# Reordering VectorE's part of a delta-rule step, and moving a gate from GpSimd to VectorE, in a one-core attention and experts kernel

## The reference

```python
def step(S, inp):                       # S: [b, h, 16, 16], 8 x 16 = 128 of them
    qt, kt, vt, at, gkt = inp
    S = S * jnp.exp(gkt)[..., None]
    sab = jnp.einsum('bhk,bhkv->bhv', at, S)
    S = S + kt[..., None] * (sab[..., None, :] + vt[..., None, :])
    ot = jnp.einsum('bhk,bhkv->bhv', qt, S)
    return (S, ot)
...
_, o = jax.lax.scan(step, S0, seq)      # 512 steps, one after the other
...
o = o * jax.nn.sigmoid(x @ Wog1 @ Wog2) # the gate of the outputs
...                                     # layer norm of o, @ Wo
out = out + cw[:, e:e + 1] * y          # eight experts, top 2 of each token
...
g = _silu(_L0_ffn_ref(xn, ...))
x = x + s * g
```

## Time and profile before

| | |
|---|---|
| runs | 1128.91, 1129.39, 1130.73 us; median 1129.39 us |
| profiled execution | 1127.93 us, of which the span of its instructions 1126.2 us |
| VectorE busy | 1067.1 us, 95% of the span |
| GpSimd busy | 924.9 us, 82% |
| TensorE busy | 898.2 us, 80% |
| ScalarE busy | 462.3 us, 41% |
| chain that ended last | VectorE 67%, issue 14%, GpSimd 9% |

### The profile page before, as it was taken

The page is one execution under the profiler, slowest core; times in us unless marked ns, Lnnn a source line. Parts: engine busy times, 40 slices in busy tenths (PEclk is TensorE's granted clock), DMA queues, the critical chain, the costliest instruction groups (busy, mean ns, idle before and its releaser), DMA issues.

```text
span 1126.2 us, 17298 instructions
## 1 busy us (share of the span) xinstructions
PE 898.2 (80%) x3893; PEld 703.1 (62%) x3893; DVE 1067.1 (95%) x3292; ACT 462.3 (41%) x1182; POOL 924.9 (82%) x921
## 2 busy tenths in 40 slices
PE   5899979312539999999989999999999962687761
PEld 3444434112528888888878888888888852566641
DVE  3899999999999999999999999999999999999994
ACT  5878858400003333333333333333333310788761
POOL 3887757447766899999989999999999998999993
PEclk9989979655769999999999999999999985888985
DMA  5656566666235767766767776666666615556322
GB/s 160 199 178 226 177 204 199 227 189 199 90 113 151 214 210 219 212 195 203 216 177 219 215 219 210 203 200 213 212 206 204 199 42 150 161 158 196 102 69 65
DMA packets 238292, 202.76 MB, mean 180 GB/s; under 512 B 140528, under 2 KB 216272, under 8 KB 238224
## 3 DMA queue, kind: packets, MB, share of 16 engines
q1 hardware_dynamic: 161184, 82.93, 27.4%
q10 hardware_dynamic: 70224, 100.49, 26.9%
q0 software_dynamic: 6816, 18.69, 4.7%
HBM read 139.54 MB, written 62.54 MB: 179 GB/s over the span
## 4 chain that ended last, share of the span: by engine, by line
DVE 67%; issue 14%; POOL 9%; SPq 4%; DMA 3%; PE 2%; ACT 1%; DVEq 0%; POOLq 0%; ACTq 0%
DVE obh L1324 9%; DVE psB L1382 7%; DVE state L1398 6%; DVE ubuf L1387 5%; DVE outer L1395 5%; DVE psB L1385 5%; DVE psB L1393 5%; POOL prod_a L370 3%; DVE ubuf L1340 3%; POOL prod_q L387 3%; DVE prod_a L1333 3%; DVE prod_q L1388 2%; DVE psB L1390 2%; SPq L395 2%; DMA rec_d<-work 2%
## 5 line engine op out<-in xcount | busy, mean ns | idle before, releaser
L370 POOL TENSOR_TENSOR prod_a<-state,rbh 128x512 f32<-128x512 f32 x203 | 258.9, 1275 | 58.4 <-DVE state L1398 43.0
L1015 PE MATMUL psA<-xT,wts 128*128 128x256 f32 x1248 | 284.3, 385 | 8.3 <-ACT work L809 7.5
L1026 PE MATMUL psF<-wts,work 128*128 128x256 f32 x1248 | 275.8, 379 | 0.0
L1015 PEld LDWEIGHTS psA<-xT,wts 128*128 128x128 f32 x1248 | 238.1, 192 | 48.3 <-ACT work L809 14.6
L1026 PEld LDWEIGHTS psF<-wts,work 128*128 128x128 f32 x1248 | 234.2, 190 | 30.3
L387 POOL TENSOR_TENSOR prod_q<-state,rbh 128x512 f32<-128x512 f32 x178 | 226.2, 1271 | 0.0
L1324 DVE TENSOR_REDUCE obh<-prod_q 128x16 f32<-128x272 f32 x480 | 204.2, 426 | 0.0
L809 ACT ACTIVATE work<-psA,b_sb 128x256 f32<-128x256 f32 x312 | 130.2, 472 | 168.8 <-PE psA L1015 142.8
L820 ACT ACTIVATE work<-psF,work 128x256 f32<-128x256 f32 x78 | 37.0, 474 | 196.9 <-PE psF L1026 196.9
L548 POOL TENSOR_TENSOR rinv<-ssm,neghalf 128x16 f32<-128x16 f32 x32 | 98.2, 3069 | 2.7
L1398 DVE TENSOR_TENSOR state<-psB,outer 128x256 f32<-128x256 f32 x203 | 86.2, 424 | 7.0
(11 more groups left out here) (195 smaller groups left out, 1558.5 us busy)
## 6 DMA issues: line engine op xcount, KB each, us to landing
wts<-in_L_ffn_W_dram ACTq DMA_DIRECT2D x78, 1024.0 KB, 5.6
rec_d<-work SPq DMA_DIRECT2D x32, 768.0 KB
rbh<-rec_d SPq DMA_DIRECT2D x32, 768.0 KB, 6.3
xs_d<-zero SPq DMA_DIRECT2D x26, 387.0 KB, 10.5
work<-xs_d ACTq DMA_DIRECT2D x39, 258.0 KB, 5.5
wts<-y_d ACTq DMA_DIRECT2D x16, 512.0 KB, 5.7
x_acc<-in_L_attn_x_dram SPq DMA_DIRECT2D x32, 128.0 KB
o_d<-obh SPq DMA_DIRECT2D x32, 128.0 KB, 7.8
```

The lines of the kernel that those rows point to most:

```text
L370: eng.tensor_tensor(prod_a[:, n, 1:3, :, 0:HD], state[:, g % SR, :, :].unsqueeze(1).broadcast_to(wide), rows.unsqueeze(2).broadcast_to(wid ...
L1015: mm = pe.matmul(psA[m // 2 % 2][:, m % 2 * MT:(m % 2 + 1) * MT], w1_sb[v][:, c, m * P:(m + 1) * P], xgT[:, c, :], start=(c == 0), stop=(c ...
L1026: mm = pe.matmul(psF[q][:, 0:D], hT[:, m, q * P:(q + 1) * P], w2_sb[v][:, m, :], start=(m == 0), stop=(m == FC - 1))
```

## The change

In `two_shared_steps` the sum over GpSimd's product (`raw`) is put ahead of the outer product into `home_o`, and the small product into `prod_q` behind the second outer product, ahead of the new state. The constants of the waits follow the new order. The gates of chunks 7 to 26 leave GpSimd's queue and stand in VectorE's, ahead of pair 3 of the chunk after each; those of chunks 27 to 30 stay with GpSimd. Two constants of the scatters' plan and the pairs that may scatter change too.

```diff
-LAND0, LAND_STEP, LAND_LAG = 390.0, 15.0, 6.0
-PAIR_STEP = 3.72
+LAND0, LAND_STEP, LAND_LAG = 390.0, 14.8, 6.0
+PAIR_STEP = 3.6
 PARTS, LAST_PARTS = (0, 4, 6), (2, 6, 7)
-SCATTERS = (1, 2, 5, 7)
+SCATTERS = (1, 3, 5, 7)
...
-                if g % NP == GATED and g // NP > SHARED:
+                if g % NP == GATED and g // NP >= WOVEN:
                     pool.wait_ge(s_o, summed(g // NP * RING - 1))
                     gate_outputs(pool, g // NP - 1)
...
                 sum_row(g - 2, 1)
+                dve.wait_ge(s_dec, g + 1)
+                dve.tensor_reduce(raw, prod_a[:, n, 2, :, :], AX.X, ALU.add).then_inc(s_chain, 1)
                 dve.wait_ge(s_chain, done + 2)
                 dve.tensor_tensor(home_o, over_v(rbh[:, u, 2 * n, K_:K_ + HD]), over_k(u1), ALU.mult).then_inc(s_chain, 1)
-                dve.wait_ge(s_dec, g + 1)
-                dve.tensor_reduce(raw, prod_a[:, n, 2, :, :], AX.X, ALU.add).then_inc(s_chain, 1)
-                dve.tensor_scalar(prod_q[:, g % SR, 1, :, HD], u1, pair[:, 0, n:n + 1], None, ALU.mult).then_inc(s_chain, 1)
-                dve.wait_ge(s_chain, done + 4)
+                dve.wait_ge(s_chain, done + 3)
                 dve.scalar_tensor_tensor(out=u2, in0=u1, scalar=pair[:, 1, n:n + 1], in1=raw, op0=ALU.mult, op1=ALU.add)\
                     .then_inc(s_chain, 1)
-                dve.wait_ge(s_chain, done + 3)
+                dve.wait_ge(s_chain, done + 4)
                 dve.tensor_tensor(home_o, prod_a[:, n, 1, :, 0:HD], home_o, ALU.add).then_inc(s_chain, 1)
-                dve.wait_ge(s_chain, done + 6)
+                dve.wait_ge(s_chain, done + 5)
                 dve.tensor_tensor(outer[:, 1, :, :], over_v(rbh[:, u, 2 * n + 1, K_:K_ + HD]), over_k(u2), ALU.mult)\
                     .then_inc(s_chain, 1)
-                dve.wait_ge(s_chain, done + 8)
+                dve.tensor_scalar(prod_q[:, g % SR, 1, :, HD], u1, pair[:, 0, n:n + 1], None, ALU.mult).then_inc(s_chain, 1)
+                dve.wait_ge(s_chain, done + 7)
                 dve.tensor_tensor(new, home_o, outer[:, 1, :, :], ALU.add).then_inc(s_chain, 1)
...
-                    for done in range(max(0, c - 2), min(c, SHARED)):
+                    for done in range(max(0, c - 2), min(c, WOVEN - 1)):
                         if gate_after(done) == c * NP + n:
                             dve.wait_ge(s_o, summed((done + 1) * RING - 1))
```

## The result

The changed kernel is slower: 1134.99 us (median of 20 runs, 1130.86 to 1137.66) against 1130.69 us for the kernel before (20 runs, 1126.48 to 1136.07). The medians differ by 4.3 us; the ratio, taken over all runs, is 1.0031, with a 95% interval of 1.0019 to 1.0043, that is +3.5 us (2.1 to 4.9). The prediction had +3.7 us. The profiled execution took 1131.92 us with a span of 1130.2, 4.0 us more than before.

A forecast was written before the change was run, and what follows sets the result against it. VectorE was taken to set the pace from pair 53 to about 220. The terms -0.7 - 0.5 + 0 + 4.9 + 0 = +3.7 us on the median 1129.39 gave 1133.1 us, range 1128 to 1137.5.

The forecast's parts named there:

- The pair: In each pair with GpSimd on time: state to state 3.45 us against 3.56, saving 0.11 us.
- The waits after scatters: VectorE waits 0.23 or 0.35 us after scatters of pairs 1, 5; 0.12 or 0.24 after 3; pairs 64 to 219: 0.
- The gate: Moved gate ahead of pair 3 costs VectorE 0.21 us; GpSimd's product held until 0.61 us after state instead of 0.51.
- The schedule: Early half tiles one pair later save 0.5 us; last scatter in pair 217 makes GpSimd and VectorE wait, +4.9 us.
- The tail: From pair 221 on: taken as 0, with bounds of 3.9 us saved and 2 us lost.
- The sum: Whole kernel: -0.7 - 0.5 + 0 + 4.9 + 0 = +3.7 us.
- pairs 53 to 63: Stretch with no moved gate: 1.2 us saved, two waits of 0.24 and 0.23 back, in all -0.7 us.
- (1): No stall at pair 220, so not slower: -1.2 us, 1128.2 us; chance 0.11.
- (2): GpSimd doesn't hold VectorE up after scatters: chunk 28.7 us, -10.8 us, 1118.6 us; chance 0.08.
- (3): Moved gate holds GpSimd to the gate's end, in 20 chunks: +3 us, 1136 us; chance 0.17.
- (4): Moved gate doesn't hold GpSimd at all, in 20 chunks: -2 us, 1131 us; chance 0.14.
- (5): Small product hides nothing, pairs stay at 3.56 us: chunk about 30.0, 1145 us; chance 0.07.

The follow-up runs named there:

- Experiment 5: Kernel before with only the small product moved ahead of the state: 1146.95 us, ratio 1.0011 to the kernel before on the second chip.
- experiment 4: Changed kernel, its gates of chunks 7 to 26 multiplying by home_o in PSUM, so one SBUF input: 1134.68 us, ratio 1.0028 to the kernel before.
- experiment 1: Changed kernel with every tile due from pair 185 on, last scatter in pair 215 instead of 217: 1130.24 us, ratio 0.9992 to the kernel before.
- experiments 6 and 7: Experiment 6, and the same with the middle chunks' gates back on GpSimd in pair 2; the second took 1131.22 us, ratio 0.9885 to the kernel before.
- Experiment 6: Changed kernel with the last scatter earlier and the old order in pairs where GpSimd is late: 1133.86 us, ratio 0.9900 to the kernel before.
- experiment 8: Changed kernel with the last tile's two scatters in pairs 217 and 219 instead of 215 and 217: 1159.14 us, ratio 1.0128 to the kernel before.

## Why the prediction was right, point by point

**The pair.** State to state 3.44 us on time, predicted 3.45. The small product's spacing at its new place, which no row of before showed, is 0.14 (607.96 to 608.10): the value taken. Experiment 5 adds what the prediction's sum had in it without saying so, that the small product's move is worth nothing without the other.

**The waits after scatters.** Before pair 220 they come behind pairs 1, 3 and 5 as worked out, and nowhere else: 17, 10 and 19 of 0.15 us and more. They are a little longer: pairs of 3.70 and 3.81 on time values of 3.44 are delays of 0.26 and 0.37, against 0.23 and 0.35; behind the gate pair 0.16 and 0.28, against 0.12 and 0.24. Over 19.5 chunks that is the term that came out worst: chunks of 29.52 or 29.63 where 29.42 or 29.54 was worked out, so pairs 64 to 219 cost about +2.3 us (the 1.54 above, with 0.78 for the early scatters added back) where 0 was taken, just over the upper bound of +2. A tenth of a microsecond a chunk is three delays off by about 0.03 each: the sum over GpSimd's product starts 1.31 to 1.33 us after L370, not 1.30, and it does so three times in a chunk.

**The gate.** +0.21 us, exact. GpSimd's product is held for 0.11 to 0.12 us, predicted 0.10. The Trainium skill, page "SBUF — State Buffer", section "SBUF: two separate sides", has the pair of ports locked for the whole instruction; the trace agrees that there is a hold, and experiment 4 that it needs the second SBUF input, but its length is not that of the instruction as the profile shows it. The gate starts at 627.38 and lasts 0.42, and L370's 0.12 us too many from 627.54 put the release at 627.66, 0.28 after the gate's start; in the earlier trace rows it was 0.27.

**The schedule.** At the early end the two pairs that had held GpSimd back (99 and 107, 4.12 and 3.91 us before) fell to 3.64, which is 0.75 to 0.8 us against the 0.5 predicted from one of them. At the late end the last scatter fell in pair 217, the chain lasts 15.75 us (15.6 predicted) and the stall cost 5.4 us (4.9 predicted). It is the largest term, and experiment 1 shows that it is the whole difference between slower and no change.

**The tail.** -0.8 us where 0 was taken from bounds of -3.9 and +2. Besides the stall VectorE waits 13 times there, 6.8 us, against 6 times and 2.8 before; the shorter pairs make up for that and a little more.

**The sum.** The terms that came out dearer (chunks +2.3, stall with pair 220 +0.4, pairs 53 to 63 +0.2) outweigh those that came out cheaper (tail -0.8, early scatters -0.3): 5.5 us by the profile from pair 53 on, against 3.7 predicted. The runs' 3.5 us lies on the prediction, closer than its terms would have brought it; by the profiles it should have come out up to 2 us higher. The mechanisms are shown; that last agreement is partly luck.

**The rivals.** (1), no stall, is refuted by the 5.23 us ahead of L611. Experiment 1 makes that case true by hand: its ratio of 0.9992, -0.9 us with an interval of -3.1 to +1.2, holds the -1.2 that the rival was priced at, while its profile from pair 53 on has +1.0. (2), no hold-up after scatters, fell with the 9.9 us in 46 waits before pair 220; experiments 6 and 7 show that most of what it would have given could be had. (3) and (4), a hold to the gate's end or none, are both refuted: 0.11 to 0.12 lies where the earlier trace rows had it, and experiment 4 is what "none" looks like. (5), pairs that stay at 3.56, is refuted by 3.44; in experiment 5 pairs do stay at 3.56, but there because the gap ahead of u2 opens.

## What to carry to other kernels

A consumer moved earlier in one engine's queue spends the producer's slack; set that slack against every lateness in the producer's queue (here scatters and casts) before counting the gain, and if it is spent only in some iterations, keep the old order in those (experiments 6 and 7, with the last scatter earlier: 0.3% of loss on one chip, 1.0% and 1.15% of gain on the other). A plan that is written in iterations has to be read again at its last item when an iteration changes length, since the last transfer one slot later can end in a wait that everything stands behind. Of two instructions that could fill a gap, see which gap they leave where they came from.

## What was not expected of the hardware

The second chip loses 11 to 15 us in pairs 47 to 49, in all four profiles taken there and in none of the first chip's. The code there is the same in every kernel. Two of the waits of experiment 5 in that stretch (us, times, longest):
```profile
PE psB L1036 <- issue: 16.7, 5, 11.6
DVE rbh L1292 <- remote: 4.7, 1, 4.7
```
They are put down to "issue" and "remote", nothing that the profile records of this core's own work. The kernel before is 13.3 us slower on that chip too (1144.94 against 1131.61), so the ratios stand, but what causes it is open. Experiments 6 and 7 were compared there only, and their times gain more (11 and 14 us) than the pairs from 53 on do in the profiles (7 and 11); that remainder isn't explained. Part of it can lie in the comparison with the other chip: against experiment 5's profile, which is of the same chip, the pairs after 53 are 9.0 and 13.0 us shorter. Experiment 6's profile is of the slowest of its six runs, but what it had lost (some 7 us against the other three) lies ahead of pair 53.

A scatter's landing isn't of one length. From the start of the last scatter to the loads that wait for it, it was 2.47 to 2.49 us in nine profiles and 4.94 in experiment 8, with other transfers begun just ahead of it. The twenty scatters of a kernel that stand 2.5 us behind SyncE's load L430 take 4.1 to 6.8 us to land in every profile with the new plan; of the others in the change 18 take 2.7 to 6.3 as well, so those transfers can't be all of it.

Where two programs are the same word for word, ahead of pair 53, one profiled execution was 1.56 us ahead of the other. So a term smaller than that is read between two points of one profile, and not from the difference of two spans.
